# A graph network megakernel on one core: adjacency writes taken out of the rows stage and spread over the stages ahead of it

## What is computed

```python
x = x + _L0_gnn_ref(_layernorm(x), edge_index, edge_attr_32, ...)   # 4 GINE layers
x = x + _L0_ffn_ref(_layernorm(x)[None], ...)[0]                    # half of the tokens, picked by a ranking
x = x + _L1_gnn_ref(_layernorm(x), W, attn_src, attn_dst, edge_index, edge_type)   # relational attention
x = x + _L1_ffn_ref(...)[0]                                         # one expert per token
x = x + _L2_gnn_ref(_layernorm(x), edge_index, edge_weight, ...)    # graph convolution, twice
x = x + _L2_ffn_ref(...)[0]
x = x + _L3_gnn_ref(_layernorm(x), edge_index, edge_weight, ...)    # graph convolution, once
x = x + _L3_ffn_ref(...)[0]
```

## Time and profile before

| | |
|---|---|
| Three runs, median (lowest to highest) | 4837.89 us (4830.57 to 4844.03) |
| The profiled execution, its own time | 4816.76 us |
| Its span, first to last instruction | 4815.1 us |
| Busy: PE, PE's weight loads, DVE, ACT, POOL | 2940.5, 2371.2, 2290.0, 868.0, 1824.1 us |
| Sends of the adjacency (L488), 264 | 264.7 us on POOL, 1002 ns each |
| Gathers of the GINE layers (L833), 1056 | 1003.6 us on POOL, 950 ns each |

### The profile page before, as it was taken

The page is one execution under the profiler, slowest core; times in us unless marked ns, Lnnn a source line. Parts: engine busy times, 40 slices in busy tenths (PEclk is TensorE's granted clock), DMA queues, the critical chain, the costliest instruction groups (busy, mean ns, idle before and its releaser), DMA issues. The chain is left out here.

```text
span 4815.1 us, 58214 instructions
## 1 busy us (share of the span) xinstructions
PE 2940.5 (61%) x16851; PEld 2371.2 (49%) x16852; DVE 2290.0 (48%) x6653; ACT 868.0 (18%) x2228; POOL 1824.1 (38%) x1982
## 2 busy tenths in 40 slices
PE   3566756675667566606405945673949829948392
PEld 3455545554555455405304723333948729937382
DVE  7666556665665566652202436784154421134113
ACT  1122212221222222202001310000310103310020
POOL 4366446645663566342472036651010020020212
PEclk8788878887888788857557956775979959979696
DMA  6633223322332333215001213332947539945594
GB/s 163 207 90 91 69 76 89 90 62 84 90 90 53 91 90 90 48 37 181 18 1 46 89 45 89 95 71 81 335 156 240 186 103 331 327 161 171 176 334 133
DMA packets 357404, 599.03 MB, mean 124 GB/s; under 512 B 81862, under 2 KB 239864, under 8 KB 354808
## 3 DMA queue, kind: packets, MB, share of 16 engines
q1 hardware_dynamic: 245816, 357.76, 22.2%
q0 software_dynamic: 88640, 214.25, 15.6%
q10 hardware_dynamic: 22656, 23.54, 1.5%
HBM read 499.63 MB, written 95.75 MB: 124 GB/s over the span
## 5 line engine op out<-in xcount | busy, mean ns | idle before, releaser
L833 POOL DMA_INDIRECT gine_got<-gine_table,src x1056 | 1003.6, 950 | 672.7 <-issue 269.2
L890 PE MATMUL gine_p_sum<-gine_hot,gine_got 128*128 128x128 f32 x4224 | 843.9, 332 | 537.7 <-issue 209.6
L890 PEld LDWEIGHTS gine_p_sum<-gine_hot,gine_got 128*128 128x128 f32 x4224 | 690.3, 232 | 731.1 <-issue 622.3
L919 DVE TENSOR_TENSOR gine_got<-gine_got,gine_p_edge 128x256 f32<-128x256 f32 x1056 | 440.3, 417 | 563.2 <-PE gine_p_edge L881 336.8
L898 ACT ACTIVATE gine_got<-gine_got 128x256 f32<-128x256 f32 x1056 | 439.8, 416 | 1182.2 <-issue 690.4
L927 DVE TENSOR_TENSOR stack_acc<-stack_acc,gine_p_sum 128x256 f32 x1056 | 437.7, 415 | 3.5
L2219 POOL DMA_INDIRECT edge_space<-h_table,hrow x264 | 262.6, 995 | 386.1 <-issue 329.9
L488 POOL DMA_INDIRECT adjacency<-value,place x264 | 264.7, 1002 | 311.9 <-POOLq L54 133.9
L842 DVE TENSOR_SCALAR gine_hot<-iota_free,dst 128x128 f32<-128x128 f32 x1056 | 348.8, 330 | 60.2 <-issue 29.2
L880 PE MATMUL gine_p_edge<-gine_w_a,edge_space 128*128 128x256 bf16 x1056 | 331.7, 314 | 34.7 <-DVEq L910 17.4
L1365 PE MATMUL ffn_p_h<-ffn_xt,ffn_w 128*128 128x128 f32 x2864 | 347.5, 279 | 0.9 <-DMA ffn_w<-in_L_ffn_w 0.4
(11 more groups left out here) (398 smaller groups left out, 3537.1 us busy)
## 6 DMA issues: line engine op xcount, KB each, us to landing
gcn_a<-adjacency SPq DMA_DIRECT2D x270, 320.0 KB
ffn_w<-in_L_ffn_W SPq DMA_DIRECT2D x74, 1024.0 KB
ffn_w<-in_L_ffn_w SPq DMA_DIRECT2D x60, 1024.0 KB
ffn_w<-in_L_ffn_w SPq DMA_DIRECT2D x90, 512.0 KB
adjacency<-zero_row ACTq DMA_DIRECT2D x3, 7200.0 KB, 43.7
gine_got<-gine_table,src POOLq DMA_INDIRECT x1056
h_table<-score_rows SPq DMA_DIRECT2D x15, 1056.0 KB
adjacency<-zero_row SPq DMA_DIRECT2D x1, 7200.0 KB, 28.1
```

Source lines behind the costliest of these rows:

```text
L833: pool.indirect_dma_start(got[:, c % RING, :], None, table, bass.IndirectOffsetOnAxis(ap=rows[:, c:c + 1], axis=0)).then_inc(gathered[c % ...
L890: ins = nc.tensor.matmul(p_sum[d % 4][:, half * P:(half + 1) * P], got[:, d % RING, half * P:(half + 1) * P], hot[:, d % HOTS, :], start=T ...
L919: nc.vector.tensor_tensor(got[:, c % RING, :], got[:, c % RING, :], p_edge[c % 4][:, 0:D], ALU.add).then_inc(summed, 1)
```

## The change

Only the counts change. The 170 sends of the rows stage go to the stages ahead of it; the total stays 264 (before: 4 x 4 + 3 x 6 + 10 + 30 + 6 + 14 + 170; after: 4 x 25 + 3 x 17 + 22 + 53 + 12 + 26 + 0).

```diff
--- before.py
+++ after.py
@@ -951,7 +951,7 @@
 
         @block.gpsimd
         def _(pool):
-            g.adj.send(pool, 4)
+            g.adj.send(pool, 25)
 
         @block.tensor
         def _(pe):
@@ -1016,13 +1016,13 @@
         L = i["L0_gnn_W1"].shape[0]
         for k in range(L):
             table = g.dram(f"gine_table{k}", [NP, D])
-            affine = {} if k == 0 else dict(gamma=i["L0_gnn_gamma"][k, :], beta=i["L0_gnn_beta"][k, :], relu=True, stats=stats, edges=6)
+            affine = {} if k == 0 else dict(gamma=i["L0_gnn_gamma"][k, :], beta=i["L0_gnn_beta"][k, :], relu=True, stats=stats, edges=17)
             layernorm(nc, g, g.X if k == 0 else h, y, table=table, addrow=i["L0_gnn_eb"][k, :], turned=acc,
                       eps=i["L0_gnn_eps"][k:k + 1], **affine)
             gine_edges(nc, g, table, i["L0_gnn_eW"][k, :, :], acc)
             gine_mlp(nc, g, acc, h, i["L0_gnn_W1"][k, :, :], i["L0_gnn_b1"][k, :, :], i["L0_gnn_W2"][k, :, :],
                      i["L0_gnn_b2"][k, :], first=(k == 0), stats=stats)
-        layernorm(nc, g, h, y, gamma=i["L0_gnn_gamma"][0, :], beta=i["L0_gnn_beta"][0, :], relu=True, add=g.X, stats=stats, edges=10)
+        layernorm(nc, g, h, y, gamma=i["L0_gnn_gamma"][0, :], beta=i["L0_gnn_beta"][0, :], relu=True, add=g.X, stats=stats, edges=22)
 
 
 class Routes:
@@ -1061,7 +1061,7 @@
 
         @block.gpsimd
         def _(pool):
-            g.adj.send(pool, 30)
+            g.adj.send(pool, 53)
 
         @block.tensor
         def _(pe):
@@ -1768,7 +1768,7 @@
         def _(pool):
             nc.gpsimd.iota(chunk[:, :], [[1, EC + PADS]], base=0, channel_multiplier=0,
                            allow_small_or_imprecise_dtypes=True).then_inc(chunk_made, 1)
-            g.adj.send(pool, 14)
+            g.adj.send(pool, 26)
 
         @block.tensor
         def _(pe):
@@ -1900,7 +1900,7 @@
         def _(pool):
             nc.gpsimd.iota(rel_idx[:, :], [[1, R]], base=0, channel_multiplier=0,
                            allow_small_or_imprecise_dtypes=True).then_inc(iota_made, 1)
-            g.adj.send(pool, 170)
+            g.adj.send(pool, 0)
 
         @block.tensor
         def _(pe):
@@ -2374,7 +2374,7 @@
             xt = inner.sb("xt", [P, T, 2, P])
             with Phase(nc, "rgat_ln") as first:
                 xn = first.sb("xn", [P, T, D])
-                layernorm(nc, g, g.X, xn, turned=xt, edges=6)
+                layernorm(nc, g, g.X, xn, turned=xt, edges=12)
             relation_scores(nc, g, xt, i["L1_gnn_W"], i["L1_gnn_attn_src"], i["L1_gnn_attn_dst"], score_src, score_dst, order)
             relation_rows(nc, g, score_src, score_dst, scores, xt, i["L1_gnn_W_turned"], h_table)
         acc = ph.sb("acc", [P, T, WIDE])
```

## The result

The changed kernel takes **4717.7 us** (median of 4 runs, 4709.9 to 4726.6), the kernel before beside it 4837.8: a ratio of 0.9753, 95% interval 0.973 to 0.9775. That is 120 us less, where 180 were forecast; the time lies 13 us above the top of the range, 4705. The profiled execution took 4720.1 us.

The account below looks back on a forecast made before the run. Sends were taken to occupy, 1.40 us each, something that engines need for their next instruction. Terms -208 + 12 + 2 + 3 + 1.5 + 9 = -180 us from 4816.8 give 4637; plus 21 to the median, 4658 us, range 4634 to 4705.

Parts of the forecast that it names:

- Rows stage, -208: Rows stage: without its 170 sends the first two passes run freely, 208 us less, bounds 200 to 212.
- Dense parts, +2: Four dense parts with 25 sends each: sends end barely past the stage, PE's supply costs nothing; 2 us more.
- 83 cover 61, so I cost it at nothing: Dense part: 38 matmuls supplied at 0.364 us each plus a reserve of 45 cover PE's last 61.
- a partial form: Rival: only the dense parts' PE runs dry, 10 us in each, 4698 us; chance 0.09.
- Relation stage, +9: Relation stage: 12 more sends prolong PE's poor supply to near 2315; 9 us more, bounds 0 and 16.
- Last normalisation, +12: Stack's last normalisation: 22 sends, 5.3 us of waiting beside DVE's two-source operations, POOL ends it; 12 us more.
- DVE is held by the sends: Rival: sends keep DVE's two-source operations waiting in the touched stages, 21 us, at most 53; chance 0.06.
- Ranking, +1.5: Ranking: 53 sends end at 2138.7, DVE at 2137.2; 1.5 us more, with no starving of DVE.
- the walk: Send-by-send timing of POOL: 1.28 us each, longer for one that starts during a DVE operation on two SBUF tensors.
- Layers' normalisations, +3: Three layers' normalisations, 17 sends each: small overrun and a slower last table write; 3 us more together.
- The starvation moves along: Rival: sends starve engines wherever they stand, 223 us lost against 208 gained, 4853 us; chance 0.04.
- the two slow passes: Rival: the rows stage's first two passes are slow from another cause and stay so, 4866 us; chance 0.02.

Follow-up runs that it names:

- e15: The changed kernel, complete, on the second kind of chip, against the kernel before there: 4311.2 us, ratio 1.0048.
- the third chip: The changed kernel run once more, complete, beside the kernel before on another chip: 4690.1 us, ratio 0.9731.
- e2: The changed kernel with 12 sends instead of 25 in each dense part, the other 52 left out: 4664.3 us.
- e1: The changed kernel with all 264 adjacency sends left out: 4606.0 us.

## Why the prediction was wrong, step by step

- **Rows stage, -208: right** (-210.5), and PE's clock is 0.80 over the first two passes and 0.92 after, both nearer the 2.4 GHz level than the 0.53 of before; I had looked for 0.85 in the first.
- **Dense parts, +2: the step that failed** (+52.7). As the prediction put it, "83 cover 61, so I cost it at nothing". The reserve and the rate were taken from another stage as if they were PE's, and the reserve was set against the part's last 13.8 us, 20 us after its first send, as if nothing had drawn on it till then. What the runs showed in their place: 32 matmuls in 15.5 us, where the sum had 83 for 13.8; 12 sends cost 0.8 us, 25 cost 14.0; DVE goes dry as well as PE, and each stops the other, since PE's buffers are freed by DVE; and the rate of 0.364 us for a matmul is no constant, but was read at the end of a short shortage. The text named the condition ("or DVE's own instructions take from the supply"), and the rival "a partial form" priced it at 10 us a part; it was 13 (52.7 for the four), and the chance of 0.09 was much too low for a cover that rested on one stretch of one other stage.
- **Relation stage, +9: too small** (+14.4), inside its bounds. Here the same constant fails: 0.84 us for a matmul in a shortage of 21 us.
- **Last normalisation, +12: right** (+13.5), and so is its mechanism. POOL ends it; beside DVE's two-source operations of 2108.18 and 2115.64 stand sends of 1.52 and 2.18 us. The Trainium skill (SBUF — State Buffer, section Who interferes with whom) infers that writing descriptors isn't held by such an operation, and says that a GpSimd instruction that reads SBUF is. The sends are held, as before. They also need an index list that lies in SBUF, so the trace speaks against the inference only if this list isn't what waits, and no run here tells the two apart. Of the rule in the same section of the Trainium skill, that the later of the two waits for the whole instruction, only one half shows: the send waits, DVE doesn't (its operation of 2110.02 starts while the send of 2109.26 runs). The rival "DVE is held by the sends" falls with that: from the start of DVE's first such operation in this stage to the end of the last it is 17.0 us, with 22 sends and with none.
- **Ranking, +1.5: too small** (+6.9). In this trace that isn't starving: DVE has no gap of it, and on the other kind of chip the stage grows by 6.7 as well. The sends end where the walk put them, 72.1 us after the stage began, for 71.0. What I left out is the way out of a stage that POOL ends:

```profile
2216.82 0.17 DVE L1106 SCALAR_TENSOR_TENSOR cap_gate<-rank_rank,rank_w 128x15 f32<-128x15 f32 x1
...
2222.34 0.97 POOL L488 DMA_INDIRECT adjacency<-value,place  x1 [0.30 <-issue]
2228.58 0.97 POOL L1268 DMA_INDIRECT cap_slots<-cap_xn,cap_slot  x1 [5.27 <-PEq L54]
```

  5.3 us from the last send's end to the next stage's first instruction on POOL, where 0.9 lay between DVE's end and it before. In the last normalisation it is 2.4 us for DVE, in the dense part of e15 2.6 (POOL's last send ends at 1776.3). On the third chip and in e2 the other term failed too, the starving that I had costed at nothing: the same 53 sends give 102.4 and 103.8 us.
- **Layers' normalisations, +3: right in size** (+3.8), in part by luck. The second one's last send ends 26.8 us after the stage's start, about where the walk put it, and the next stage starts 2.1 us later: the way out again. That makes up its 28.9 us, for 27.1 with no sends, and leaves nothing for the slower table write that I had charged. **Attention's normalisation, 0:** 2.8 us with the feed-forward ahead of it.
- The rivals: "The starvation moves along" needed 208 us of loss and got 94, not all of it starving; the two slow passes did have the sends as their cause (e1: none without them).
- Not on my list at all was that the price of a send differs from chip to chip. The forecast's nine tenths for "faster" took no account of that; on the second kind the right answer was "slower by 0.5%".

## What to carry to other kernels

Here a run of indexed transfers cost next to nothing at first (12 sends 0.8 us) and 1.0 us each after (13 more 13.2 us), like a queue that is filled faster than it is emptied. So put a few of such transfers in many places (12 here, 2 at a time in a loop) rather than many in some, and read how many a stage bears by halving them there once, not from another stage. Where a stage is itself full of such transfers none is free (1.35 us each beside the gathers). Look at the untouched transfers first: gathers each 1.48 us where their engine needs 1.25 came with the starving on every chip here, 1.25 with none: a gain measured beside the one may not be there beside the other.

## What the runs showed of the hardware

- Two kinds of chip: the kernel before takes 4816 to 4838 us on at least three of them and 4280 to 4289 on two; its gathers of 128 rows of 1 KB start each 1.46 to 1.48 us on the one kind and 1.25 on the other, and only on the first do indexed transfers starve the engines. No run came back to a chip, and what a chip's other cores did meanwhile is on no record, so whether this belongs to the chip or to its state at that time isn't shown.
- There, index lists of 128 rows starve PE and DVE alike, with 4 or 512 bytes a row written or 4 read: 238 us for 170 of them. That they do so by holding back the engines' instructions is my reading of the "issue" idle time in straight-line code; the server itself is in no view.
- POOL, when it ends a stage on an indexed transfer, hands over 2.1 to 5.3 us later, on both kinds; where DVE ended it, POOL began 0.9 us later.
